# A four-layer attention kernel: the low parts of the feed-forward weights are made on GpSimd instead of VectorE, a wait is taken off the bias additions, and one stage of a hand-written order is given another time

## The reference, cut to what matters

```
q  = (latents @ q_w + q_b)            # 16 heads of 16
kv = (concat([x, latents]) @ kv_w + kv_b)
attn = softmax(where(mask, q k^T / 16, -inf))
h = (attn v) @ out_w + out_b + residual
h = rmsnorm(h, postnorm_w)
out = gelu(h @ mlp_w1 + mlp_b1) @ mlp_w2 + mlp_b2 + residual     # 256 -> 1024 -> 256
```

## Time and profile before

| | |
|---|---|
| median of 3 runs | 2287.4 us (2283.65 to 2288.02) |
| the profiled execution, its time | 2288.02 us |
| its span | 2286.0 us |
| TensorE busy with matmuls | 94% |
| TensorE weight loads | 78% |
| VectorE | 64% |
| ScalarE | 56% |
| GpSimd | 29% |

### The profile page before, as it was taken

One profiled execution on the slowest core, in us unless ns is written; L12 is line 12 of the kernel. 1 busy time (PEld: TensorE's weight loads), 2 busy tenths in 40 slices (PEclk: granted clock), 3 DMA queues, 4 the chain that ended last, 5 costly groups with the idle time before them and its releaser, 6 DMA issues. The chain is left out here.

```text
span 2286.0 us, 47737 instructions
## 1 busy us (share of the span) xinstructions
PE 2156.8 (94%) x18208; PEld 1789.3 (78%) x18208; DVE 1467.7 (64%) x2828; ACT 1277.9 (56%) x3300; POOL 651.6 (29%) x661
## 2 busy tenths in 40 slices
PE   6999979999896999999999999999998899999899
PEld 4666646888685888888888888888887786776678
DVE  5888854555444766665666666666666439999963
ACT  4777754565543454444445444444444548888863
POOL 4444320111125421020303312030101217677711
PEclk9999999999998999999999999999998899999999
DMA  4000020000102000010100000000000211000000
GB/s 134 16 16 11 2 57 1 2 2 2 38 1 79 24 24 24 15 32 10 38 1 24 24 22 26 10 29 1 1 1 37 75 29 30 2 2 2 2 10 29
DMA packets 33662, 50.59 MB, mean 22 GB/s; under 512 B 2592, under 2 KB 22048, under 8 KB 32416
## 3 DMA queue, kind: packets, MB, share of 16 engines
q1 hardware_dynamic: 33440, 47.53, 6.8%
HBM read 45.43 MB, written 2.10 MB: 21 GB/s over the span
## 5 line engine op out<-in xcount | busy, mean ns | idle before, releaser
L690 ACT ACTIVATE l_probs<-l_s_psum,l_neg_max 128x129 f32<-128x129 f32 x512 | 181.5, 368 | 266.8 <-DVE l_neg_max L753 266.8
L777 DVE TENSOR_TENSOR x<-x,l_o_psum 128x512 f32<-128x512 f32 x256 | 176.1, 688 | 189.7 <-PE l_o_psum L644 188.0
L675 ACT ACTIVATE l_KT<-l_k_psum,cols 128x512 f32<-128x512 f32 x128 | 88.2, 689 | 197.3 <-PE l_k_psum L114 197.3
L1303 DVE TENSOR_REDUCE l_neg_max<-l_psum 128x2 f32<-128x512 f32 x256 | 163.4, 683 | 47.9 <-PE l_psum L1093 47.4
L522 POOL TENSOR_TENSOR l_head_w_high<-l_head_raw,one 128x768 fp32r<-128x768 f32 x30 | 44.5, 1483 | 516.2 <-PE l_o_psum L644 516.2
L2355 POOL TENSOR_TENSOR l_probs<-l_probs,l_mask_add 128x512 f32<-128x512 f32 x128 | 161.8, 1285 | 76.9 <-DVE l_probs L2583 76.9
L644 PE MATMUL l_o_psum<-l_head_w_high,l_context_low 128*128 128x256 f32 x512 | 156.1, 305 | 8.5 <-DVE l_context_low L758 8.5
L758 DVE SCALAR_TENSOR_TENSOR l_context_low<-l_c_psum,cols,l_context_high 128x512 fp32r<-128x512 f32 x128 | 95.8, 749 | 105.2 <-ACT l_context_high L682 104.5
L1232 ACT ACTIVATE l_PT<-l_psum 128x512 f32<-128x512 f32 x256 | 132.2, 603 | 54.7 <-PE l_psum L1121 54.7
L2525 ACT ACTIVATE l_probs<-l_probs,l_neg_max 128x128 f32<-128x128 f32 x512 | 159.8, 396 | 5.4 <-DVE l_neg_max L2590 4.9
L644 PE MATMUL l_o_psum<-l_head_w_high,l_context_high 128*128 128x256 f32 x512 | 144.6, 282 | 5.2 <-DVE x L777 3.1
(11 more groups left out here) (301 smaller groups left out, 6382.0 us busy)
## 6 DMA issues: line engine op xcount, KB each, us to landing
l_head_raw<-in_l_heads SPq DMA_DIRECT2D x32, 384.0 KB, 3.0
l_w<-in_l_w SPq DMA_DIRECT2D x4, 1024.0 KB, 9.3
l_ctx_in<-in_ctx_T SPq DMA_DIRECT2D x16, 256.0 KB, 5.5
l_value_raw<-in_l_values SPq DMA_DIRECT2D x8, 512.0 KB, 3.6
l_value_rows<-in_l_rows SPq DMA_DIRECT2D x8, 512.0 KB, 5.0
l_x_in<-in_x_T SPq DMA_DIRECT2D x16, 128.0 KB, 2.1
l_x_in<-in_ctx_T SPq DMA_DIRECT2D x16, 128.0 KB, 2.7
values<-in_l_w SPq DMA_DIRECT2D x2, 1024.0 KB, 5.9
```

What stands on the lines that cost most here:

```text
L690: last = act.activation(probs[:, i, :], scores[:, i // 2, i % 2, :], ACT.Exp, bias=neg_max[:, i:i + 1], scale=1.0, accum_out=den[:, i:i + 1])
L777: dve.tensor_tensor(out=x, in0=x, in1=o_bank[:, :], op=ALU.add).then_inc(o_free, 1)
L1303: dve.tensor_reduce(neg_max[:, u % 2, qt, at:at + 2], bank[:, :].rearrange("p (e k) -> p e k", e=2), AX, ALU.max, negate=True).then_inc(fr ...
```

## The change

Four edits.

1. The times of `exponents` parts 4 to 7 in `AT1` go from -3.2 to -3.18. `neg_T_a` has -4.18, so `exponents(u, 4..7)` and `neg_T_a(u+1)` now have the same time but for rounding.
2. `w1_low(1..3)` and `w2_low(0..3)` move from VectorE to GpSimd. `w1_low(0)` stays on VectorE and gets a semaphore of its own, `w1_first`, on which `up(g, 0)` and `up(g, 1)` wait.
3. In `FEED_ORDER` `w2_low(q)` now stands right behind `w2_high(q)`, ahead of the first `biased_b2`, and no longer between the `h_split` of group 0.
4. `biased_b2` no longer waits for `up(g, 7)`.

```diff
@@ AT1
-    "exponents": (-4.15, -4.11, -3.97, -3.97, -3.2, -3.2, -3.2, -3.2),
+    "exponents": (-4.15, -4.11, -3.97, -3.97, -3.18, -3.18, -3.18, -3.18),
@@ Feed.__init__
+        self.w1_first = sem("w1_first")
@@ Feed.gpsimd
+        def w1_low(q):
+            if q == 0:
+                return
+            raw, high, low = self.quarter1(q)
+            pool.wait_ge(self.w1_rounded, q + 1)
+            pool.tensor_tensor(out=low, in0=raw, in1=high.bitcast(F32), op=ALU.subtract).then_inc(self.w1_ready, 1)
+
+        def w2_low(q):
+            raw, high, low = self.quarter2(q)
+            pool.wait_ge(self.w2_rounded, q + 1)
+            pool.tensor_tensor(out=low, in0=raw, in1=high.bitcast(F32), op=ALU.subtract).then_inc(self.w2_ready, 1)
...
         def biased(b):
             x = self.c.x[:, b, :]
-            if b % 4 == 0:
-                self.filled(pool, "up", b // 4, 7)
             if self.late and b == 12:
@@ Feed.vector
         def w1_low(q):
-            raw, high, low = self.quarter1(q)
-            dve.wait_ge(self.w1_rounded, q + 1)
-            dve.tensor_tensor(out=low, in0=raw, in1=high.bitcast(F32), op=ALU.subtract).then_inc(self.w1_ready, 1)
-
-        def w2_low(q):
-            raw, high, low = self.quarter2(q)
-            dve.wait_ge(self.w2_rounded, q + 1)
-            dve.tensor_tensor(out=low, in0=raw, in1=high.bitcast(F32), op=ALU.subtract).then_inc(self.w2_ready, 1)
+            if q == 0:
+                raw, high, low = self.quarter1(0)
+                dve.wait_ge(self.w1_rounded, 1)
+                dve.tensor_tensor(out=low, in0=raw, in1=high.bitcast(F32), op=ALU.subtract).then_inc(self.w1_first, 1)
@@ Feed.tensor
         def up(g, f):
-            pe.wait_ge(self.w1_ready, f // 2 + 1)
+            if f < 2:
+                pe.wait_ge(self.w1_first, 1)
+            else:
+                pe.wait_ge(self.w1_ready, f // 2)
@@ FEED_ORDER
-FEED_ORDER += [("w2_high", _q) for _q in range(4)]
+for _q in range(4):
+    FEED_ORDER += [("w2_high", _q), ("w2_low", _q)]
 for _g in range(4):
     FEED_ORDER += [("biased_b2", 4 * _g + _n) for _n in range(4)]
     for _f in range(8):
         FEED_ORDER += [("up", _g, _f), ("gelu", _g, _f), ("h_split", _g, _f)] + LATE_AT.get((_g, _f), [])
-        FEED_ORDER += [("w2_low", _f - 1)] if _g == 0 and 1 <= _f <= 4 else []
```

More of the change, by code:

```diff
@@ L1937, in biased @@
             pool.tensor_tensor(out=x, in0=x, in1=self.c.row(self.finish), op=ALU.add).then_inc(self.x_biased, 1)
-        return {"biased_b2": biased, "late_root": late_root, "late_low": late_low,
+        return {"w1_low": w1_low, "w2_low": w2_low, "biased_b2": biased, "late_root": late_root, "late_low": late_low,
                 "early_root": early_root}
@@ L2022, in late_scaled @@
             last.then_inc(self.xn_done, 1)
-        return {"split": split, "w1_low": w1_low, "w2_low": w2_low, "h_split": h_split, "added_b2": added, "late_stats": late_stats,
+        return {"split": split, "w1_low": w1_low, "h_split": h_split, "added_b2": added, "late_stats": late_stats,
                 "late_scaled": late_scaled, "early_stats": early_stats, "early_scaled": early_scaled}
```

## The result

The changed kernel takes 2302.62 us (median of 4 runs, 2301.53 to 2304.23) against 2285.53 us for the kernel before beside it (median of 4, 2283.58 to 2288.02): ratio 1.0075, 95% interval 1.0057 to 1.0092, so 17.1 us slower. The profiled execution took 2303.46 us with a span of 2301.4 us, 15.4 us over that of before. The forecast was 2312.0, 1.1% slower, with a range of 2298 to 2328: direction and mechanisms held, and the sum of 24.6 us was too large, by 7.5 us beside the medians and by 9.2 us beside the profiled executions.

What follows compares the result with a forecast made beforehand. TensorE, busy in 94% of the span, was taken to bound the kernel. Attention stalls and clock (13.1 + 4.1), l1, l2 and l3 terms and relief summed to +24.6 us on 2288.02, so 2312 us for the median, range 2298 to 2328.

Steps and rivals of the forecast that it cites:

- stalls in `attention1`: Units 8 to 14: exponents run behind the copy, so TensorE stands still ahead of the context; +13.1 us.
- clock behind them: After long attention stalls matmuls may run at half clock, 1.66 us each; half of five taken, +4.1 us (0 to 8.3).
- start of l1: `w1_low(1)` and `(2)` on GpSimd hold up `split(0, 1)`; TensorE waits 2.2 us at half clock, worth +1.0 us.
- group 1 of l1, with the clock: Context splits on GpSimd hold up group 1's `h_split`s: about 7.7 us, plus 1.1 us for a clock that falls.
- end of l1: GpSimd is done long before, so the next block starts 7.8 us sooner.
- group 1 of l2: `early_root` no longer waits for `up(1, 7)`, but bias additions 8 to 15 follow it; gain 2.6 of a possible 5.9 us.
- last `h_split` of each group: Groups 1 to 3: without bias additions beside `h_split(g, 7)`, waits of 0.2 us go; about -1.0 us over three feed-forwards.
- The turns: GpSimd and VectorE alternate at SBUF: VectorE gets one instruction (0.55 us) for each of GpSimd's, whatever its length.
- heavier: Rival: clock falls after each stall, and GpSimd wins the first turn in l1 and l3; 2322 us, chance 0.22.
- Only the order costs: Rival: feed-forward turns are cheap, VectorE's queue catching up within the buffers; +3.5 us, 2291 us, chance 0.07.
- The table's edit changes nothing: Rival: rounding keeps the old order in the attention; +7.4 us, 2295 us, chance 0.03.
- faster: Rival: exponents' shift hidden by a transpose ready 2.4 us earlier, and cheap turns; 2274 us, chance 0.04.

Runs made afterwards that it cites:

- e1: The kernel before with only the `exponents` 4 to 7 times changed from -3.2 to -3.18: 2302.06 us, ratio 1.0065.
- e4: The kernel before with -3.18 for exponents 6 and 7 alone, 4 and 5 keeping -3.2: 2292.65 us, ratio 1.0024.
- e2: The changed kernel with the old exponent times, so the feed-forward edits alone: 2288.74 us, ratio 1.0008 to the kernel before.
- e5: e2 with the wait of the bias additions on `up(g, 7)` put back, so only the low parts are moved: 2293.57 us, ratio 1.0033.
- e3: e2 with the context split in 16 GpSimd instructions instead of 4: 2282.51 us, ratio 0.9982 to the kernel before.
- e6: The kernel before without the bias additions' wait on `up(g, 7)`, low parts left on VectorE: 2298.97 us, ratio 1.0059.
- e8: The kernel before with two context splits behind the bias additions of group 0 and two behind those of group 1: 2281.69 us, ratio 0.9977.
- e11: e8 with the context split in pieces of 128x512, as in e3: 2278.68 us, ratio 0.9965 to the kernel before.
- e9: The kernel before with each group's bias additions listed behind its last `h_split`, not ahead of its first `up`: 2280.74 us, ratio 0.9975.
- e10: e9 with the bias additions waiting for `h_split(g, 7)` instead of `up(g, 7)`: 2279.23 us, ratio 0.9966 to the kernel before.
- e12: e8 with the context's high part made by a copy instead of multiplying by a row of ones: 2280.64 us, ratio 0.997 to the kernel before.

## Why the prediction was right, and where its sum was off

| term of the sum | forecast | in the trace | shown by |
|---|---|---|---|
| stalls in `attention1` | +13.1 | +13.1 (14.76 less one drop of 1.6) | e1, e4 |
| clock behind them | +4.1 (0 to 8.3) | +1.6 (one of five; two of five in e1) | the row at 573.89, e1 |
| start of l1 | +1.0 | +2.2 (up to 1.4 is scatter) | e2, e5 |
| group 1 of l1, with the clock | +8.8 | +5.8 | e2, e3, e6 |
| end of l1 | -7.8 | -8.3 | e6, e8, e11 |
| group 0 of l2 | +3.85 | +3.0 | e2, e5 |
| group 1 of l2 | -2.6 | -2.1 (-3.6 in e2) | e9, for the whole 5.9 |
| group 0 of l3 | +5.2 | +5.7 | e2, e5 |
| last `h_split` of each group | -1.0 | about -3, what is left over | e10, in l1 |
| block behind l1, the rest | 0 | -2.1, -0.6 | chance (the table) |
| sum | +24.6 | +15.4 | |

The start of group 2 shifts by 5.35 us over that of group 1, and by then 0.48 us of relief are given back (ScalarE's `gelu(1, 7)`, at 635.26 before, shifts by 21.84), hence the 5.8. Of these 3.54 are the wait; most of the rest is the low clock behind it.

- **The order.** That 8 - 3.18 ties with 9 - 4.18, that the table's order decides, and that TensorE has nothing to fill the gap: all seen, and e4 shows the price per exponent.
- **The clock.** I took half of the possible drops. In the ten long stalls of the change's and e1's traces three were followed by matmuls at 1.2 GHz (3.52 to 3.58 us instead of 1.96), so a third. The term was of the right kind and 2.5 us too large. The Trainium skill, "TensorE: Matmul & The Clock Gate", section "Why this matters for your kernels", would have it at 0 for gaps this short; the rows at 503.82 and 573.89 disagree with it.
- **The turns.** Rows 9 and 10 carried over to instructions of 3.6 to 4.9 us: three `h_split` of the change pay one whole split each, and in e6 four VectorE instructions do. The Trainium skill, "SBUF — State Buffer", section "Who interferes with whom", says that the pair is held for the whole instruction; e8 (a cast of 3.82 us beside a split of 4.05) agrees.
- **Group 1 of l1, mis-sized by 3 us.** I had GpSimd's bias additions end at 625.0 on the axis of before. They ended when the first split began, at 637.53, which less the shift of 16.4 is 621.1. So the splits began 3.9 us sooner, the first lay beside additions from PSUM, and the last turn ended at 638.9 (655.34 less 16.4), not at 643.4. Four `h_split` were to pay; three did.
- **Start of l1, too small by 1.2 us.** I had rightly seen `split(0, 1)` held up (2.2 us forecast, 2.0 in the rows at 612.23 and 613.77), but halved it, as if a wait at the slow clock were paid back by the time `down` starts. It was not: the change, e2 and e5 have +2.1 or +2.2 and e3 +2.8 from 576 to 606, while the kernels with the quarters on VectorE and the wait in place have between -1.4 and +0.3.
- **Relief, too small by 2 us.** I priced it by TensorE's waits of 0.2 us; the shift per group is 0.37 to 0.48 in l1. The 3 us in the table are not measured as such: they are what the other terms leave of the 15.4. The wait shown is shorter than the delay, since the trace's matmul ends are modelled; steps of work are better read from starts.
- **What no term held.** The profiled execution of before had 2.1 us of low clock behind l1 that nine of the thirteen others don't have. My sum leaned on one execution; its time was 2.5 us above the median of the runs beside the change.
- **Luck.** The sum did not come near by errors that cancel: most of them made it too large. But the same way of counting turns missed e6 by 20 us, sign included, because it left out instructions that VectorE still owed. That this cost the forecast of the change little I take for luck, though no run isolates it: there the `w2_low` are off VectorE's list and the splits come 8 us later than in e6 (621.1 and 612.9 on the axis of before), with the eight `up` of group 1 ahead of what needs them.

The rivals: "heavier" fell, since the clock term was smaller still. "Only the order costs" had the feed-forwards at -13.7 us; e2 has them at +1.8. The turns are not cheap (+2.2, +5.8, +3.0 and +5.7); they are just about paid by what the removed wait gives. "The table's edit changes nothing" fell with the first timeline, "faster" with the transpose: it is at 528.16 and the copy at 528.41, 0.25 us behind it, as before (525.66 and 525.92) and not 2.4 us later.

## What to carry to other kernels

When two engines take turns at SBUF, the price of a meeting is the other's instruction length times the number of instructions that one still owes the critical engine. So put long GpSimd work where VectorE has nothing that is due, cut it into pieces, and count VectorE's whole backlog at that moment, not only the step named in the list. A wait that looks like a needless brake may be what keeps such work out of the way: here taking it off cost 12 us by itself, while moving the jobs in the list, cutting the splits in pieces and waiting for one step more gave 18 us in all.

In a list sorted by written times, treat a tie as an edit of the order; and price a moved instruction by what must now run between a late input and the work that needs it, while the engine's idle time ahead of that input is lost.

## What the runs showed of the hardware

- GpSimd is slowed as well (the changed kernel and e6): the split of 3.60 us takes 4.05 us when a VectorE instruction gets in between, 0.45 us per turn.
- A VectorE instruction with two SBUF inputs ends about 0.5 us behind the end of GpSimd's; an addition from PSUM keeps its 0.42 us beside any of them.
- A one-input copy on GpSimd holds VectorE's cast as a two-input operation does, and makes 128x2048 elements in 2.36 us where multiplying by a row of ones takes 3.60 to 4.05 (e12, e8).
- The same stall of 2.37 us was followed by the low clock (0.50 to 0.53) in three cases and not in seven (the change and e1); what decides it is not shown here. Whether a VectorE instruction with one input and without a cast would be held wasn't tried.
